# A fused attention and FP4 FFN layer: turning the FFN's activations by DMA instead of on TensorE

## What is computed

```python
# sublayer 1, a chunked linear attention over rows before t, without a softmax
v = x @ W_write.T
S[t, s] = (x[t] . x[s-1]) * gamma ** (t - 1 - s)  for s < t, else 0
z = layernorm(2 * x + alpha * (S @ v) @ W_read.T)
# sublayer 2, FFN whose operands are all rounded blockwise to FP4 (blocks of 16)
q(a) = nearest of {0, .5, 1, 1.5, 2, 3, 4, 6} of |a| / scale, with sign, * scale
       scale = max|a| over the block / 6
h = silu(q(z) @ q(w_gate).T) * (q(z) @ q(w_up).T)      # 704 wide
out = layernorm(z + q(h) @ q(w_down).T)
```

## Time and profile before

| | |
|---|---|
| median of 3 runs | 324.39 us (324.23 to 324.56) |
| profiled execution | span 322.5 us from its first to its last instruction; the page gives no other time for it |
| instructions | 6519 |
| TensorE's matmuls, its granted clock | 2067, 1.000 |
| HBM read, written | 11.08 MB, 4.19 MB |
| DMA queues | 15.69 MB, mean 49 GB/s |

### The profile page before, as it was taken

One profiled execution on the slowest core, in us unless ns is written; L12 is line 12 of the kernel. 1 busy time (PEld: TensorE's weight loads), 2 busy tenths in 40 slices (PEclk: granted clock), 3 DMA queues, 4 the chain that ended last, 5 costly groups with the idle time before them and its releaser, 6 DMA issues.

```text
span 322.5 us, 6519 instructions
## 1 busy us (share of the span) xinstructions
PE 314.5 (97%) x2067; PEld 285.2 (88%) x2067; DVE 293.0 (91%) x746; ACT 213.2 (66%) x521; POOL 238.2 (74%) x258
## 2 busy tenths in 40 slices
PE   7999999999999999999999999999999999999994
PEld 3999988989998998999989998898989889998983
DVE  4799789989899999899998999889999999999973
ACT  7769994767775647844784556766675555665664
POOL 1999898668696868676886768777779588368872
PEclk9999999999999999999999999999999999999999
DMA  6830301010010200320020200021000000001002
GB/s 227 302 125 9 132 0 67 1 66 2 1 67 16 84 16 0 100 82 3 16 83 17 83 17 3 33 65 35 1 18 17 16 18 17 19 16 35 17 33 84
DMA packets 8242, 15.69 MB, mean 49 GB/s; under 512 B 1040, under 2 KB 5136, under 8 KB 8208
## 3 DMA queue, kind: packets, MB, share of 16 engines
...
HBM read 11.08 MB, written 4.19 MB: 47 GB/s over the span
## 4 chain that ended last, share of the span: by engine, by line
PE 69%; DVE 17%; issue 5%; ACT 4%; POOL 3%; ACTq 0%; DVEq 0%; POOLq 0%
PE gu L1712 11%; PE gu L1716 11%; PE gu L1713 11%; PE bank L1817 5%; PE bank L1712 4%; PE bank L1716 4%; PE bank L1713 4%; PE bank L1722 3%; DVE h_y L1094 3%; PE bank L1725 3%; PE bank L1726 3%; DVE w_raw L1209 2%; DVE hqT_lo L1236 2%; DVE h_am L1215 2%; PE bank L1783 2%
## 5 line engine op out<-in xcount | busy, mean ns | idle before, releaser
L413 POOL TENSOR_TENSOR h_q<-h_g,h_ns 128x704 f32<-128x704 f32 x32 | 51.2, 1604 | 47.7 <-DVE h_g L1099 47.6
L1712 PE MATMUL gu<-guT_hi,xqT_hi 128*128 128x512 f32 (+1 forms) x192 | 74.0, 386 | 0.7 <-DVE w_raw L1209 0.6
L1713 PE MATMUL gu<-guT_lo,xqT_hi 128*128 128x512 f32 (+1 forms) x192 | 72.2, 376 | 0.0
L1716 PE MATMUL gu<-guT_hi,xqT_lo 128*128 128x512 f32 (+1 forms) x192 | 56.6, 376 | 0.0
L699 ACT ACTIVATE w_raw<-gu 128x512 f32<-128x512 f32 x64 | 29.3, 462 | 32.7 <-PE gu L1716 32.4
L406 POOL TENSOR_TENSOR h_n<-w_raw,h_rs 128x704 f32<-128x704 f32 x32 | 47.0, 1472 | 3.4 <-DVE h_rs L1089 3.2
L719 ACT CAST hqT_hi<-bank 128x512 fp32r<-128x512 f32 x64 | 30.4, 478 | 17.7 <-PE bank L1817 17.2
L1712 PEld LDWEIGHTS gu<-guT_hi,xqT_hi 128*128 128x128 f32 x192 | 36.1, 188 | 6.0 <-ACT xqT_hi L688 0.9
L1716 PEld LDWEIGHTS gu<-guT_hi,xqT_lo 128*128 128x128 f32 x192 | 35.5, 188 | 6.0 <-ACT xqT_lo L693 0.2
L1713 PEld LDWEIGHTS gu<-guT_lo,xqT_hi 128*128 128x128 f32 x192 | 36.1, 188 | 4.8
L1094 DVE SCALAR_TENSOR_TENSOR h_y<-h_sq,h_n 128x704 f32<-128x704 bf16 x34 | 36.9, 1090 | 0.0
...
## 6 DMA issues: line engine op xcount, KB each, us to landing
xs<-in_x_rows_dram SPq DMA_DIRECT2D x8, 512.0 KB, 3.4
out_dram<-wq_gu SPq DMA_DIRECT2D x32, 128.0 KB, 1.7
x_full<-in_xt_rows_dram SPq DMA_DIRECT2D x7, 512.0 KB, 3.2
w_raw<-in_w_ffn_dram SPq DMA_DIRECT2D x6, 352.0 KB, 6.0
w_pair<-in_w_attn_dram SPq DMA_DIRECT2D x1, 512.0 KB, 5.2
...
scal<-in_scalars_dram ACTq DMA_DIRECT2D x1, 1.0 KB, 1.7
```

Of the source, the lines that this page charges most:

```text
L413: nc.gpsimd.tensor_tensor(blocks(h_q[:, p, 0:I]), blocks(h_g[:, p, :]), per_block(h_ns[:, p, :], HB), ALU.mult).then_inc(h_quant, 1)
L1712: nc.tensor.matmul(dst, lh, rh, start=(first and i == 0), stop=False)
L1713: nc.tensor.matmul(dst, lh, rl, start=False, stop=False)
L1716: last = nc.tensor.matmul(dst, ll, rh, start=False, stop=(end and i == len(terms) - 1))
```

## The change

For tiles 0 to 29 the turn of h leaves TensorE. The grid values and the scales are turned apart and multiplied afterwards:

- `h_to_grid` writes h_g as bf16. `hg_repeat` (ScalarE) repeats its last 64 columns. SP turns all 768 columns with one transposing DMA, SBUF to SBUF, into h_gT.
- `h_divisors` writes the scales h_ns in another order (48 of 64 columns are used). `repeat_h_scales` (ScalarE) fills the repeated ones; TensorE turns them in one transpose (`h_scale_rows`); `copy_h_scales` (ScalarE) brings the 64x128 result to SBUF; SP writes it to DRAM and, when that has landed, reads it back with each row spread over 16 partitions (h_sT, 128x768 float32).
- `h_spread` (POOL) multiplies h_gT by h_sT: h_q arrives turned. `h_round_all` casts its 768 columns at once and `h_rest_all` subtracts them, both from SBUF.

Tiles 30 and 31 keep the old path. Beside that:

- Loads (`load_x_transposed` 2 to 7, `load_x` 1 to 7) and stores (0 to 30) are issued from ScalarE's list; SP's list has the initial loads, the scales, the turns and the last store.
- All squares go to PSUM, h's and the weights' over two banks. PSUM is one tensor `ps` of 8 banks, and tables give the banks of each step and tile. v_subtract, xq_subtract and the ScalarE copies behind them are gone; `v_rest` and `xq_rest` (VectorE) make all low parts.
- `gate_up` waits for silu_ready in place of h_ready ahead of the gate, and for h_ready ahead of the up half.
- `x_moments` works on one column at a time; `out_moments` leaves out the mean except for the last tile (POOL's `out_stats` takes the sum).
- The loop `body` is gone; every list is one written order of all 32 tiles. The order differs throughout, the start included.

```diff
-            load_x_transposed(2)
-            load_x(1)
...
+            def write_h_scales(k, p, turn):
+                sp.wait_ge(hs_copied, k + 1)
+                sp.dma_start(h_scales_dram[k], h_s[:, p, :]).then_inc(hs_written[p], 16)
+
+            def spread_h_scales(k, p, turn):
+                sp.wait_ge(hs_written[p], 16 * turn)
+                if turn > 1:
+                    sp.wait_ge(h_quant, k - 1)
+                sp.dma_start(h_sT[:, p, :], over_rows(h_scales_dram[k], SC, HC)).then_inc(hs_landed[p], 16)
+
+            def turn_h_grid(k, p, turn):
+                sp.wait_ge(hg_repeated, k + 1)
+                if turn > 1:
+                    sp.wait_ge(h_quant, k - 1)
+                sp.dma_start_transpose(h_gT[:, p, :, :], h_g[:, p, :]).then_inc(hg_turned[p], 16)
...
+            write_h_scales(12, 0, 7)
+            spread_h_scales(12, 0, 7)
+            write_h_scales(13, 1, 7)
+            turn_h_grid(13, 1, 7)
+            spread_h_scales(13, 1, 7)
...
+            def h_spread(k, p, turn):
+                pool.wait_ge(hs_landed[p], 16 * turn)
+                pool.wait_ge(hg_turned[p], 16 * turn)
+                if k >= 2:
+                    pool.wait_ge(hT_lo_ready, 2 * k - 2)
...
+                nc.gpsimd.tensor_tensor(h_q[:, p, :], h_gT[:, p, :, :].rearrange("p c t -> p (c t)"), h_sT[:, p, :],
+                                        ALU.mult).then_inc(h_quant, 1)
...
-                nc.scalar.activation(h_sq[:, p, :], h_n[:, p, :], ACT.Square, scale=ROOT_K).then_inc(h_square, 1)
...
+                nc.scalar.activation(two_banks(h_sq_at[k]), halves(h_n[:, p, :]), ACT.Square,
+                                     scale=ROOT_K).then_inc(h_square, 1)
...
+            def hg_repeat(k, p):
+                act.wait_ge(h_grid, k + 1)
+                nc.scalar.copy(h_g[:, p, I:HPAD], h_g[:, p, I - TAIL:I]).then_inc(hg_repeated, 1)
+
+            def repeat_h_scales(k, p):
+                act.wait_ge(h_div, k + 1)
+                ns = h_ns[:, p, 0:SROWS].rearrange("p (s e c) -> p c s e", s=2, c=SC)
+                nc.scalar.copy(ns[:, HC - 1, 1, :], ns[:, HC - 1, 0, :]).then_inc(hs_repeated, 1)
+
+            def copy_h_scales(k, p, turn):
+                act.wait_ge(hs_filled, k + 1)
+                if turn > 1:
+                    act.wait_ge(hs_written[p], 16 * turn - 16)
+                nc.scalar.copy(h_s[:, p, :], ps[0:SHELD, hs_at[k], 0:P]).then_inc(hs_copied, 1)
+
+            def h_round_all(k, p):
+                if k >= 2:
+                    act.wait_ge(down_filled, k - 1)
+                act.wait_ge(h_quant, k + 1)
+                nc.scalar.copy(hqT_hi[:, p, :], h_q[:, p, :]).then_inc(hT_hi_ready, 2)
...
+            def store(k, slot):
+                act.wait_ge(out_ready, k + 1)
+                act.dma_start(out_rows[k], o_out[:, slot, :]).then_inc(stored[slot], 16)
...
+                        dve.wait_ge(hg_turned[p], 16 * (k // 2))
...
+            def h_rest_all(k, p):
+
+                dve.wait_ge(hT_hi_ready, 2 * k + 2)
+                nc.vector.tensor_tensor(hqT_lo[:, p, :], h_q[:, p, :], hqT_hi[:, p, :].bitcast(F32),
+                                        ALU.subtract).then_inc(hT_lo_ready, 2)
...
+                for i in (2 * u, 2 * u + 1):
+                    nc.vector.tensor_scalar(z_nm[:, i:i + 1], z_sum[:, i:i + 1], -1.0 / D, None, ALU.mult)
+                    last = nc.vector.tensor_scalar(z_ve[:, i:i + 1], z_ssq[:, i:i + 1], 1.0 / D ** 3, LN_EPS, ALU.mult, ALU.add)
...
-                    pe.wait_ge(h_ready, 2 * k + half - 1)
+                    pe.wait_ge(h_ready if half else silu_ready, 2 * k + half - 1)
...
+            def h_scale_rows(k, p, free):
+                pe.wait_ge(hs_repeated, k + 1)
...
+                nc.tensor.transpose(ps[0:SHELD, hs_at[k], 0:P], h_ns[:, p, :], ident[:]).then_inc(hs_filled, 1)
```

More of the change, by code:

```diff
@@ L245, in mk_seq_postln_kernel @@
         out_rows = out.rearrange("b (i p) d -> (b i) p d", p=P)
-        def run(body):
-            for b in range(2, 5):
-                body(b)
         block = ctx.enter_context(nc.Block())
@@ L1976, in _ @@
-            run(body)
-            down(12, 0, [(v_lo_ready, 13)])
-            values(6, 1, [(hT_lo_ready, 27)])
-            h_transpose(14, 2, 0, [(o_ready, 13)])
-            xq_transpose(4, 1, [(pr_ready, 27)])
-            gate_up(17, 4, 1, 1)
+            down(0, 0, [(wT_lo_ready, 9)])
+            gate_up(5, 1, 1, 1)
+            reads(2, 1, [(h_grid, 3)])
+            values(3, 0, [(o_ready, 1)])
+            scores(3, 0, [(z_ready, 6)])
+            gate_up(6, 1, 2, 0)
+            h_scale_rows(4, 0, [(v_lo_ready, 7)])
@@ new lines, in _ @@
+            h_scale_rows(5, 1, [(h_grid, 3)])
+            gate_up(6, 1, 2, 1)
+            gate_up(7, 1, 3, 0)
+            down(1, 1, [(hs_copied, 6)])
+            down(2, 2, [(h_grid, 6)])
+            xq_transpose(2, 0, [(o_ready, 2)])
+            scores(3, 1, [(h_grid, 6)])
+            values(3, 1, [(hs_copied, 5)])
+            h_scale_rows(6, 0, [(pr_ready, 14)])
+            down(3, 3, [(xqT_lo_ready, 5)])
+            gate_up(7, 1, 3, 1)
+            gate_up(8, 2, 0, 0)
+            scores(3, 2, [(h_grid, 7)])
@@ new lines, in _ @@
+            gate_up(8, 2, 0, 1)
+            gate_up(9, 2, 1, 0)
+            reads(3, 0, [(pr_ready, 15)])
+            xq_transpose(2, 1, [(h_grid, 7)])
+            h_scale_rows(7, 1, [(o_ready, 4)])
+            gate_up(9, 2, 1, 1)
+            gate_up(10, 2, 2, 0)
+            scores(3, 3, [(xqT_lo_ready, 6)])
+            gate_up(10, 2, 2, 1)
+            h_scale_rows(8, 0, [(pr_ready, 16)])
+            down(4, 0, [(z_ready, 7)])
+            down(5, 1, [(hs_copied, 8)])
+            reads(3, 1, [(o_ready, 5)])
@@ new lines, in _ @@
+            h_scale_rows(9, 1, [(o_ready, 6)])
+            gate_up(11, 2, 3, 0)
+            scores(4, 0, [(x_grid, 7)])
+            xq_transpose(3, 0, [(z_ready, 8)])
+            values(4, 0, [(hs_copied, 10)])
+            gate_up(11, 2, 3, 1)
+            gate_up(12, 3, 0, 0)
+            scores(4, 1, [(h_grid, 11)])
+            h_scale_rows(10, 0, [(h_grid, 11)])
+            scores(4, 2, [(v_lo_ready, 9)])
+            gate_up(12, 3, 0, 1)
+            gate_up(13, 3, 1, 0)
+            reads(4, 0, [(pr_ready, 19)])
@@ new lines, in _ @@
+            h_scale_rows(11, 1, [(h_grid, 12)])
+            gate_up(13, 3, 1, 1)
+            scores(4, 3, [(hs_copied, 12)])
+            down(6, 2, [(z_ready, 9)])
+            down(7, 3, [(x_grid, 8)])
+            xq_transpose(3, 1, [(h_grid, 10)])
+            values(4, 1, [(h_grid, 13)])
+            h_scale_rows(12, 0, [(h_grid, 13)])
+            gate_up(14, 3, 2, 0)
+            reads(4, 1, [(o_ready, 7)])
+            h_scale_rows(13, 1, [(hs_copied, 13)])
+            gate_up(14, 3, 2, 1)
@@ new lines, in _ @@
+            gate_up(15, 3, 3, 0)
+            values(5, 0, [(h_grid, 14)])
+            down(8, 0, [(x_grid, 9)])
+            scores(5, 0, [(v_lo_ready, 11)])
+            scores(5, 1, [(o_ready, 9)])
+            h_scale_rows(14, 0, [(pr_ready, 21)])
+            gate_up(15, 3, 3, 1)
+            xq_transpose(4, 0, [(hs_copied, 15)])
+            down(9, 1, [(pr_ready, 22)])
+            reads(5, 0, [(h_grid, 15)])
+            gate_up(16, 4, 0, 0)
+            down(10, 2, [(xqT_lo_ready, 9)])
@@ L1994, in _ @@
[L1994 to L2002 removed]
+            scores(6, 0, [(v_lo_ready, 13)])
+            gate_up(19, 4, 3, 1)
+            xq_transpose(5, 0, [(h_grid, 18)])
@@ L2023, in _ @@
+            h_scale_rows(22, 0, [(h_grid, 22)])
+            down(18, 2, [(xqT_lo_ready, 12)])
+            xq_transpose(6, 0, [(z_ready, 14)])
+            values(7, 0, [(hs_copied, 23)])
+            scores(7, 0, [(h_grid, 23)])
+            scores(7, 1, [(h_grid, 23)])
+            scores(7, 2, [(v_lo_ready, 15)])
+            values(7, 1, [(pr_ready, 29)])
             gate_up(23, 5, 3, 1)
-            down(18, 2, [(hT_lo_ready, 38)])
-            h_transpose(20, 0, 0, [(z_ready, 16)])
+            down(19, 3, [(pr_ready, 31)])
```

2486 lines of the change are left out of this document (1423 added, 1063 removed).

## The result

| | before | after |
|---|---|---|
| median | 324.49 us (324.23 to 324.93, 7 runs) | 320.66 us (319.53 to 323.33, 7 runs) |
| ratio to before, 95% interval | | 0.9903 (0.9882 to 0.9923) |
| profiled execution, its span | 322.5 us of span | 319.53 us, span 317.8 us |
| matmuls | 2067 | 1911 |
| HBM read | 11.08 MB | 22.87 MB |

The gain is 3.8 us by the medians (3.1 by the ratio). The sign was right, and the result lies inside the range of 304 to 338, but outside the forecast's own 306 to 319; of the 12.4 us between 324.4 and 312 less than a third came. Medians and ratios in this document leave out runs more than 1.5% above the fastest of their kernel: five of extra_turn's ten, two of double_turn's four, and one of tail_fix's four (498.89 us, TensorE granted 0.56 throughout).

What follows compares the result with a forecast made beforehand. TensorE was taken as the bound, VectorE right behind. From 324.4 us, TensorE's 12.4 and VectorE's 3.5 less and ScalarE's 1.0 more gave 309.5; 2.7 back at the end made 312 us, range 304 to 338 (forecast's own 306 to 319).

Steps and rivals of the forecast that it cites:

- TensorE's queue: TensorE, all 32 tiles: turning and subtraction matmuls go, scale transposes come; 17.9 us less, 0.56 us a tile.
- the squares from PSUM: VectorE's two rounding passes: squares read from PSUM take 0.886 us each, 6.5 and 2.4 us less over 32 tiles.
- the issue on ScalarE: ScalarE's queue: each load or store issue holds it 0.38 us, 44 of them 16.7 us more.
- the turn: DMA queue, each tile: the transposing copy of h lands after 3.4 us; from 5.0 us the DMA sets the pace.
- the subtraction of 768 elements out of SBUF: VectorE, low part of h: one subtraction of 0.93 us, 4.7 us less over 30 tiles, at worst 6 us back.
- The first 60 us: Start of the kernel, order of weights shuffled: left at zero because TensorE does the same work.
- The tail: End of the kernel: tile 29's DMA turn lands uncovered, 3.4 us in place of six matmuls; 2.7 us come back.
- The weights: Chain shares applied to each engine's saving: TensorE 69%, VectorE 17%, ScalarE 4%; 12.4 and 3.5 us less, 1.0 more.
- Rival A: Whole kernel: the new order fits the shorter TensorE queue and all 17.9 us arrive, 306.5 us; chance 0.17.
- B: Steady loop: DMA engines become the bound; at 6.0 us a turn 12 us more, 336 us; chance 0.18.
- C: Each tile: ScalarE is late with the SiLUs, copies and issues add 33 us; 331 us at three quarters; chance 0.15.
- D: Whole kernel: nothing gained, TensorE's freed queue time goes to waits for VectorE, 324 us; chance 0.12.

Runs made afterwards that it cites:

- extra_turn: The changed kernel with each of the 30 DMA turns issued a second time, into a spare buffer that no tile waits for; 327.91 us.
- double_turn: The changed kernel with each turn made twice into the same buffer, the second after the first has landed, all waits for both; 375.35 us.
- tail_fix: warm_all with other PSUM banks and an earlier place for tile 30's squares, and eight zero matmuls behind a later wait; 320.49 us, run again 319.29 us.
- warm_all: The changed kernel with matmuls of zeros filling TensorE's idle times at the start (ahead of combine too) and in the tail; 316.14 us.
- no_spread: The changed kernel without the writes and spreads of the scales of tiles 2 to 29, multiplying with those of tiles 0 and 1; 319.51 us.
- neither reordering above: Against warm_all: tail_fix, 320.49 us, and a run moving only POOL's multiplication of tile 30 ahead of the spread of tile 29's scales, 316.7 us.
- stores_sp: The changed kernel with the 31 output stores issued from SP in place of ScalarE; 319.91 us, ratio 0.9864 to the kernel before.

## Why the prediction was wrong

**Terms that held.** TensorE's queue (17.9 us, 18.0 by the counts of the stages), the squares from PSUM (priced 886, measured 883 and 878 ns), x's passes, POOL's multiplication (1.75 priced, 1.73), ScalarE's cast (0.80, 0.84), the issue on ScalarE (0.38, mostly 0.34 to 0.35), the turn (3.4, 3.9; its bound of 5.0 wasn't reached in the median). The DMA share in the loop is 0.49, under 0.8. VectorE fell by 14.1 us, not 20.6: the subtraction of 768 elements out of SBUF takes 1118 ns, not 930, so 30 x 0.19 = 5.6 us came back. The prediction had named this cost ("it may suffer what the squares suffered"), put its worst at 6 us, and left it out of the sum.

**The step that failed first** is the sentence in brackets: "The first 60 us, where the order of weights is shuffled, I leave at zero: TensorE does the same work." TensorE does the same work, at another place and at another clock. The list of the start was rewritten; I hadn't compared the two lists, and so missed that `reads(0, 1)` now stands where POOL isn't ready, and `combine` ahead of the scores that covered its load. An estimated 8.5 us of queue left the start, and only 0.8 us of time. The clock's part is shown: filling the holes at start and tail gave 4.5 us (warm_all), of the 8.7 between 312 and 320.66. The rest is, by the balance of the stages, TensorE standing still in start and tail; that another order of the lists would give it back was not run.

**The tail**, priced at 2.7 us for one landing that nothing covers, took 5.1, and here the mechanism was wrong, not only the size. The last turn took 7.59 us, not 3.4, because it met its own spread: without the spreads it landed after 3.7. But that shortened the tail by 0.4 us only (no_spread). 1.7 of the 5.1 are the clock (warm_all). The remaining 3 us come with the new order of tiles 29 to 31; which step of it costs them stays open, since neither reordering above tests it cleanly.

**The weights** (69% TensorE, 17% VectorE, from the chain) gave the right sign for a reason that isn't general. The runs show 4.0 us for 13.2 left out on TensorE alone in the old order, 10.9 for 14 added in the new one, and 26 for 25.3 more on VectorE, with POOL's 29.6 beside them. Two engines with 99 and 95% of the loop aren't a sum of shares: relief of one counts until the other binds. The change relieved TensorE's queue by a net 9.5 us and VectorE by 15 us (243.9 to 229.0) in the loop together, and so nearly all of it came. Rival A's mechanism was the true one in the loop; it was my forecast that took 69% where its own sentence "unless the order around it adapts" applied.

**The rivals.** B (DMA bound) didn't happen, but extra_turn shows that it isn't far. By the Trainium skill's 1309 ns for a block (VectorE: DVE Perf Modes, The three transpose paths) six would take an estimated 7.9 us; the turn of six lands after 2.8 us in a quiet queue (no_spread) and 3.9 beside the spreads, so the measurement decides against adding the blocks up. C (ScalarE late) is false: TensorE idles 2.2 us in the whole loop, where C began to decide at 16.5, and stores_sp puts the stores' part at 2.6 us at most. The Trainium skill says that issuing engines share the same sixteen DMA engines (DMA: Bandwidth & Descriptors, Rules for kernel authors); stores_sp agrees, where moving the stores bought nothing. D is false by the loop's 9.0 us.
